# Attention on one core: the weighting and summing of three spans' exponentials moved from VectorE to TensorE and ScalarE

## The chip, the cores and the metric

The kernel runs on one core of a Trainium2 chip. The time is the device time of one execution in microseconds (us), from the first to the last instruction and what lies around them; the figure given for a kernel is the median of several runs.

## What is computed

The reference is a chain of six layers over eight images of 1024 tokens with 128 channels: a deformable convolution, a correlation layer that sorts each token's 1024 correlations, a windowed attention, a mixture of eight experts, a state space layer and a second mixture of experts. All is float32. The change is in the attention, which for each token looks at the last 4, 16 and 32 tokens:

```python
WINDOW_SIZES = (4, 16, 32)
q = hidden_states @ Wq + bq
contexts = []
for window in WINDOW_SIZES:
    patches = _gather_patches(hidden_states, window)
    keys = patches @ Wk + bk
    values = patches @ Wv + bv
    scores = jnp.einsum('bld,blwd->blw', q, keys) * scale
    attn = jax.nn.softmax(scores, axis=-1)
    contexts.append(jnp.einsum('blw,blwd->bld', attn, values))
merged = contexts[0]
for c in contexts[1:]:
    merged = merged + c
merged = merged / len(contexts)
return hidden_states + merged @ Wo + bo
```

## The kernel before

Tokens lie on the 128 partitions. An image is two halves of 512 tokens, four tiles of 128 each. Four chains of work run at the same time, each a Python generator per engine, and each engine runs its pieces strictly in the order in which they were written:

- F: the first layer of the next image (gathers by GpSimd, `diag` weights by ScalarE at L639, products by TensorE at L597), its normalization and the correlations of both halves (L623 to L630).
- S: the sort of one half (`dve_S`, L785 to L936). It is VectorE's alone. Its last instruction, L936, writes `tc`, the input of the attention of that half.
- C: attention, first expert layer and state space layer of one half, on TensorE, ScalarE and VectorE in turns. It runs under the sort of the next half. Its last instructions on VectorE are those of L1553, which write `tm`.
- M: the second expert layer of the two halves of the image before, one after the other (L1581 to L1713). VectorE multiplies there at L1713.

How the chains' pieces follow each other on an engine is a table of letters, `ORDER`, with a string for each engine and each kind of period: `fill`, `early`, `full`, `late` and `drain`. `weave` takes the next piece of the chain whose letter stands next. `full` is used for images 1 to 6 (images 2 to 6 are a loop on the chip). In such a period VectorE sorts the two halves of image i, the C chain does the second half of image i-1 and then the first half of image i, and the M chain does both halves of image i-1. In `drain` the sort is over, and the last half's C and M chains run out.

In the attention of a half, each tile's scores lie over 160 keys (32 past ones, `BACK`, and the tile's own 128). VectorE adds the three spans' bands and takes the minimum (L1126, L1128), in two parts p of two tiles each. ScalarE takes the exponentials into `sm` and their sums into `asum` (L1105). VectorE inverts the sums (L1133), multiplies the first span's exponentials by them (L1135) and adds the two others (L1140) into `prob`, whose first 96 columns ScalarE had set to zero (L1079). TensorE transposes `prob` in blocks of 128 x 128 (L1037), ScalarE copies the result to `prob_t` (L1111), and TensorE multiplies by the values `v_tok` of the tile and of the tile before (L1046, L1047). In the traces all of these tiles are `arena`, and PSUM tiles are `bank`.

## Time and profile before

| | |
|---|---|
| median of 3 runs | 4932.3 us (4931.25 to 4941.95) |
| profiled execution, its time | 4926.9 us |
| its span, first to last instruction | 4925.1 us |
| VectorE (DVE) busy | 4278.7 us, 87% of the span |
| TensorE (PE) busy | 3975.1 us, 81% |
| ScalarE (ACT) busy | 2954.3 us, 60% |
| GpSimd (POOL) busy | 894.7 us, 18% |
| mean granted TensorE clock | 0.893 |

Shares over the whole span mix the fill, the periods in which a sort runs, and the drain. The stretches are therefore to be read apart: the first sort starts at 249 us of the span and the last one ends at 4601 us.

### The profile page before, as it was taken

The page shows a single profiled execution, that of the slowest core. Times are in us where ns is not written, and L with a number is a line of the kernel's source. Part 1 is how long each engine was busy: PE and PEld are TensorE (multiplying, and loading weights), DVE is VectorE, ACT ScalarE, POOL GpSimd, SP SyncE. Part 2 cuts the span into 40 slices and gives each one's busy share as a digit, 9 for nine tenths or more (in the row PEclk, how much of TensorE's full clock was granted, in tenths as well). Part 3 has the DMA queues.
Part 4 walks back from the last instruction along what each step waited for, and adds up shares of the span by engine and source line. Part 5 has one row for each costly group of instructions (what it writes and reads, how often), then busy time and mean ns, then how long its engine had stood idle before and what let it go on. Part 6 is the DMA issues. An engine that isn't in the chain of part 4 may idle for free.

```text
span 4925.1 us, 59870 instructions
## 1 busy us (share of the span) xinstructions
PE 3975.1 (81%) x19410; PEld 2674.8 (54%) x19410; DVE 4278.7 (87%) x5380; ACT 2954.3 (60%) x7241; POOL 894.7 (18%) x580
## 2 busy tenths in 40 slices
PE   5747748989798988989798988989798987767587
PEld 3616424667456654567456654566456653545354
DVE  1098999999999999999999999999999999999521
ACT  4526526687467846687467846687467855555452
POOL 2317000242005300242005300242005210000000
PEclk8878869999899988999799988999799988978798
DMA  4314100232013210232013210232013210010001
GB/s 131 98 35 124 35 0 18 75 101 69 5 43 110 79 36 18 75 102 68 7 43 110 79 36 18 67 104 67 13 43 109 71 40 13 22 29 27 10 22 39
DMA packets 226079, 269.71 MB, mean 55 GB/s; under 512 B 26831, under 2 KB 188506, under 8 KB 225626
## 3 DMA queue, kind: packets, MB, share of 16 engines
q0 software_dynamic: 46080, 151.03, 10.6%
q1 hardware_dynamic: 179674, 114.65, 7.9%
q8 instruction: 167, 2.74, 0.2%
q14 instruction: 158, 1.29, 0.1%
HBM read 242.25 MB, written 23.34 MB: 54 GB/s over the span
## 4 chain that ended last, share of the span: by engine, by line
PE 38%; DVE 33%; issue 12%; ACT 9%; DMA 4%; POOL 3%; SPq 1%; DVEq 0%; another core or an unknown queue 0%; ACTq 0%; POOLq 0%
PE bank L597 6%; PE bank L1633 4%; PE bank L1628 4%; PE bank L1613 3%; PE bank L1298 3%; POOL gath L759 3%; DMA gath<-quads,idx 3%; DVE srt_b L873 2%; DVE srt_b L881 2%; DVE srt_a L796 2%; DVE srt_b L796 2%; PE bank L569 2%; PE bank L1225 2%; PE bank L1218 2%; DVE srt_a L893 2%
## 5 line engine op out<-in xcount | busy, mean ns | idle before, releaser
L759 POOL DMA_INDIRECT gath<-quads,idx x576 | 894.5, 1553 | 3083.4 <-DVE idx L722 2005.3
L597 PE MATMUL bank<-diag,gath 128*128 128x128 f32 x4608 | 612.4, 295 | 167.6 <-DMA gath<-quads,idx 166.8
L639 ACT ACTIVATE diag<-ident,w 128x128 f32<-128x128 f32 x2304 | 704.6, 393 | 20.3 <-DVE w L737 20.2
L597 PEld LDWEIGHTS bank<-diag,gath 128*128 128x128 f32 x4608 | 591.3, 210 | 203.1 <-DMA gath<-quads,idx 126.9
L1613 PEld LDWEIGHTS bank<-e2w,act 128*128 128x128 f32 (+1 forms) x3072 | 409.8, 198 | 161.7 <-issue 157.3
L1628 PE MATMUL bank<-mu_t,e2w 128*128 128x512 f32 (+1 forms) x768 | 424.0, 635 | 86.4 <-DMA e2w<-moe_w_t 39.9
L1633 PE MATMUL bank<-gated_u,e2w 128*128 128x512 f32 (+1 forms) x768 | 426.1, 638 | 34.2 <-DVE act L1713 31.9
L1713 DVE TENSOR_TENSOR act<-act,bank 128x512 f32<-128x512 f32 (+1 forms) x384 | 261.3, 680 | 180.0 <-PE bank L1633 159.5
L1613 PE MATMUL bank<-e2w,act 128*128 128x128 f32 (+1 forms) x3072 | 415.0, 282 | 1.6 <-DVE act L1713 1.6
L873 DVE TENSOR_TENSOR srt_b<-srt_a 128x1024 f32<-128x1024 f32 x192 | 351.3, 1830 | 1.2
L881 DVE TENSOR_TENSOR srt_b<-srt_a 128x1024 f32<-128x1024 f32 x192 | 351.0, 1828 | 0.0
L1681 ACT ACTIVATE act<-bank 128x512 f32<-128x512 f32 (+1 forms) x384 | 227.7, 593 | 201.5 <-PE bank L1628 198.8
L1681 ACT ACT_TABLE_LOAD x199 | 255.3, 1283 | 11.9 <-PE bank L1628 8.8
L672 ACT ACTIVATE cols<-bank 128x384 f32<-128x384 f32 x192 | 93.0, 484 | 245.1 <-PE bank L597 235.7
L1633 PEld LDWEIGHTS bank<-gated_u,e2w 128*128 128x128 f32 (+1 forms) x768 | 131.3, 188 | 186.7 <-issue 140.0
L794 DVE TENSOR_TENSOR srt_b<-srt_a 128x2048 f32<-128x2048 f32 x96 | 219.6, 2287 | 1.4
L794 DVE TENSOR_TENSOR srt_a<-srt_b 128x2048 f32<-128x2048 f32 x96 | 219.5, 2286 | 0.9
L796 DVE TENSOR_TENSOR srt_a<-srt_b 128x2048 f32<-128x2048 f32 x96 | 219.2, 2284 | 0.0
L796 DVE TENSOR_TENSOR srt_b<-srt_a 128x2048 f32<-128x2048 f32 x96 | 219.2, 2283 | 0.0
L901 DVE TENSOR_TENSOR srt_a<-srt_b 128x2016 f32<-128x2016 f32 (+1 forms) x96 | 211.8, 2206 | 0.9
L903 DVE TENSOR_TENSOR srt_a<-srt_b 128x2016 f32<-128x2016 f32 (+1 forms) x96 | 211.7, 2205 | 0.0
L1628 PEld LDWEIGHTS bank<-mu_t,e2w 128*128 128x128 f32 (+1 forms) x768 | 122.1, 188 | 148.3 <-issue 62.1
(348 smaller groups left out, 8161.5 us busy)
## 6 DMA issues: line engine op xcount, KB each, us to landing
e2w<-moe_w_t SPq DMA_DIRECT2D x256, 170.5 KB
quads<-xn_tok SPq DMA_DIRECT2D x256, 64.0 KB
e1w<-L_ffn_w SPq DMA_DIRECT2D x256, 64.0 KB, 1.9
e2w<-moe_w_t SPq DMA_DIRECT2D x256, 64.0 KB
gath<-quads,idx POOLq DMA_INDIRECT x576
e2w<-moe_w_t SPq DMA_DIRECT2D x128, 42.5 KB
x_tok<-x SPq DMA_DIRECT2D x8, 512.0 KB, 4.1
out<-tm SPq DMA_DIRECT2D x16, 256.0 KB, 2.3
```

What stands on the lines that cost most here:

```text
L597: ins = T.matmul(FB[q % 2][:, k * P:(k + 1) * P], gath[:, g % 2, k, s * C:(s + 1) * C], diag[:, g % 2, 4 * k + s], start=(s == 0), stop=(s ...
L639: ins = SC.activation(diag[:, g % 2, n], ident[:], ACT.Copy, scale=w[:, n:n + 1])
L759: pool.indirect_dma_start(gath[:, g % 2, k], None, quads, bass.IndirectOffsetOnAxis(idx[:, TG * g + k:TG * g + k + 1], 0)).then_inc(sem["g ...
L794: V.tensor_tensor(dst[:, :, 0:size // 2], lo, hi, ALU.max)
L796: return V.tensor_tensor(dst[:, :, size // 2:size], lo, hi, ALU.min)
L873: V.tensor_tensor(out_lo, lo, hi, ALU.max)
L881: link.put(V.tensor_tensor(out_hi, lo, hi, ALU.min))
L1613: ins = T.matmul(MB[2][:, t * P:(t + 1) * P], act2[0:m, n % ACT2_SLOTS, t * P:(t + 1) * P], e2w[0:m, e % 2, W2 + k * C:W2 + (k + 1) * C], ...
L1628: T.matmul(MB[r % 2][0:m, :], e2w[:, e % 2, k * P:k * P + m], mu_t[:], start=True, stop=True).then_inc(sem["m_ps"], 1)
L1633: T.matmul(MB[r % 2][0:m, :], e2w[:, e % 2, W3 + k * P:W3 + k * P + m], gated_u[:], start=True, stop=True).then_inc(sem["m_ps"], 1)
L1681: SC.activation(act2[0:m, n % ACT2_SLOTS], MB[r % 2][0:m, :], ACT.Silu).then_inc(sem["m_sb"], 1)
L1713: V.tensor_tensor(act2[0:m, n % ACT2_SLOTS], act2[0:m, n % ACT2_SLOTS], MB[r % 2][0:m, :], ALU.mult).then_inc(sem["hh"], 1)
```

## The change

VectorE keeps the reciprocals alone. ScalarE multiplies the identity by each tile's and span's reciprocals, which gives twelve diagonal matrices of 128 x 128 for a half (`pdiag`). TensorE multiplies the exponentials by these: with `sm` as the stationary operand and the diagonal as the moving one, the product is the weighted exponentials transposed, and three products added in PSUM are the sum over the spans. Since the past keys are now 32 rows, and no longer the last 32 of 128, the values of the tile before are needed at partitions 0 to 31. TensorE computes them a second time (`v_past`, four products with 32 columns of weights), and ScalarE copies them; the zeroing of `prob` falls away. The copy to `prob_t` becomes two copies for each part. Fourteen strings of the `ORDER` table, nearly all in which the C chain stands beside others, are new; the first line of one is shown.

```diff
     ACT_early=(
         "FFFFFFFFFFFFFFFFFFFFFFFFFFFFFFFFFFFFFFFFFFFFFFFFFFFFFFFFFFFFFFFFFFFFFFFFFFFFFFFFFFFFFFFFFFFFFFFF"
-        "FFFFFFFFFFFFFFCFFFFCCFFCFFCCCFFFFFCCFFFCCFCCFCCFFCCFFFFFFFFFFFFCCCCCCCCCCCCCCCCCCCCCCCCCCCCCCCCC"
+        "FFFFFFFFFFFFFFCFFFCFFCFFFCCCFFCFFCCCCFFCCFCCFCCFFCCFCFFFFFFFFFFCFCFCCCCCCCCCCCCCCCCCCCCCCCCCCCCCC"
...
-        v_halo = sb("v_halo", [P, C])
+        v_halo = sb("v_halo", [BACK, C])
...
-        prob = carve(UT * 2 * P, UT, 2 * P)
+        pdiag = carve(UT * NW * P, UT * NW, P)
+        v_past = carve(HALF, UT, C)
...
@@ pe_att
                 ins = T.matmul(CB[0][:, t * P:(t + 1) * P], utile(t), wqkvo[:, 2], start=True, stop=True)
             ins.then_inc(sem["qkv"], 1)
             yield
+            pe.wait_ge(sem["qkv_sb"], unit("qkv_sb", i, h, 3))
+            for t in range(UT):
+                ins = T.matmul(CB[0][0:BACK, t * P:(t + 1) * P], utile(t)[:, P - BACK:P], wqkvo[:, 2], start=True, stop=True)
+            ins.then_inc(sem["qkv"], 1)
+            yield
             pe.wait_ge(sem["qkv_sb"], unit("qkv_sb", i, h, 2))
...
                 pe.wait_ge(sem["probd"], unit("probd", i, h, p + 1))
                 if p == 0:
-                    pe.wait_ge(sem["prob_z"], unit("prob_z", i, h))
-                    pe.wait_ge(sem["qkv_sb"], unit("qkv_sb", i, h, 3))
-                for t in range(2):
-                    for s in range(2):
-                        ins = T.transpose(CB[p][:, (2 * t + s) * P:(2 * t + s + 1) * P], prob[:, 2 * p + t, s * P:(s + 1) * P], ident[:])
+                    pe.wait_ge(sem["qkv_sb"], unit("qkv_sb", i, h))
+                for t in range(2 * p, 2 * p + 2):
+                    for k, n, at in ((0, BACK, 0), (BACK, P, P)):
+                        for w in range(NW):
+                            ins = T.matmul(CB[p][0:n, t % 2 * 2 * P + at:t % 2 * 2 * P + at + P], sm[:, t, w, k:k + n],
+                                           pdiag[:, t * NW + w], start=(w == 0), stop=(w == NW - 1))
                 ins.then_inc(sem["prob_ps"], 1)
...
-                    past = v_tok[:, t - 1] if t else v_halo[:]
+                    past = v_past[0:BACK, t - 1] if t else v_halo[:]
                     if t or h:
-                        T.matmul(out, past, prob_t[:, t, 0:P], start=True, stop=False)
+                        T.matmul(out, past, prob_t[0:BACK, t, 0:P], start=True, stop=False)
@@ act_att
-            SC.activation(prob[:, :, 0:P - BACK], ident[:, 0:P - BACK].unsqueeze(1).to_broadcast([P, UT, P - BACK]), ACT.Identity,
-                          scale=0.0).then_inc(sem["prob_z"], 1)
-            yield
...
+            act.wait_ge(sem["qkv"], unit("qkv", i, h, 4))
             if h == 0:
-                SC.activation(v_halo[:], CB[0][:, HALF - P:HALF], ACT.Identity)
-            SC.activation(flat(v_tok), CB[0][:], ACT.Identity).then_inc(sem["qkv_sb"], 1)
+                SC.activation(v_halo[:], CB[0][0:BACK, HALF - P:HALF], ACT.Identity)
+            SC.activation(flat(v_past)[0:BACK], CB[0][0:BACK, :], ACT.Identity).then_inc(sem["qkv_sb"], 1)
             yield
...
             for p in range(2):
+                act.wait_ge(sem["arec"], unit("arec", i, h, p + 1))
+                for n in range(2 * NW * p, 2 * NW * (p + 1)):
+                    ins = SC.activation(pdiag[:, n], ident[:], ACT.Copy, scale=arec[:, n // NW, n % NW:n % NW + 1])
+                ins.then_inc(sem["probd"], 1)
+                yield
+            for p in range(2):
                 act.wait_ge(sem["prob_ps"], unit("prob_ps", i, h, p + 1))
-                SC.activation(flat(prob_t[:, 2 * p:2 * p + 2]), CB[p][:], ACT.Identity).then_inc(sem["prob_sb"], 1)
+                two = CB[p][:].rearrange("p (t s q) -> p t s q", t=2, s=2)
+                SC.activation(prob_t[0:BACK, 2 * p:2 * p + 2, 0:P], two[0:BACK, :, 0], ACT.Identity)
+                SC.activation(prob_t[:, 2 * p:2 * p + 2, P:2 * P], two[:, :, 1], ACT.Identity).then_inc(sem["prob_sb"], 1)
                 yield
@@ dve_att
                 dve.wait_ge(sem["expd"], unit("expd", i, h, p + 1))
-                two = range(2 * p, 2 * p + 2)
-                link(V.reciprocal(arec[:, 2 * p:2 * p + 2], asum[:, 2 * p:2 * p + 2]))
-                for t in two:
-                    ins = V.tensor_scalar(prob[:, t, P - BACK:2 * P], sm[:, t, 0], arec[:, t, 0:1], None, ALU.mult)
-                link(ins)
-                for w in (1, 2):
-                    for t in two:
-                        y = prob[:, t, P - BACK:2 * P]
-                        ins = V.scalar_tensor_tensor(y, sm[:, t, w], arec[:, t, w:w + 1], y, ALU.mult, ALU.add)
-                    if w == 1:
-                        link(ins)
-                ins.then_inc(sem["probd"], 1)
+                V.reciprocal(arec[:, 2 * p:2 * p + 2], asum[:, 2 * p:2 * p + 2]).then_inc(sem["arec"], 1)
                 yield
```

In the rows of the changed kernel below, line numbers are those of its own text. On VectorE, at the first attention of the loop's period (the second half of image i-1, under the sort of image i), the order before is this; L808 and L810 are pieces of the sort, L1126 and L1128 the bands and minima, L1133 to L1140 the weighting, and L1161 to L1163 the router of the M chain:

```order
L1126 TENSOR_TENSOR arena<-bank,band 128x960
...
L1128 TENSOR_REDUCE arena<-arena 128x6
...
L1161 SCALAR_TENSOR_TENSOR mgv<-moh,ml 128x32
...
L808 TENSOR_TENSOR corr<-srt_b 128x4x3x128
L810 TENSOR_TENSOR corr<-srt_b 128x4x3x128
L1133 RECIPROCAL arena<-arena 128x6
...
L1135 TENSOR_SCALAR arena<-arena 128x160 x2
...
L1140 SCALAR_TENSOR_TENSOR arena<-arena 128x160 x2
```

At the same place in the changed kernel (L809, L811, L795 and L797 are the sort, L1141 and L1143 the bands and minima, L1147 the reciprocals, L1156 and L1160 the router):

```order
L809 TENSOR_TENSOR corr<-srt_b 128x4x3x128
L811 TENSOR_TENSOR corr<-srt_b 128x4x3x128
...
L1141 TENSOR_TENSOR arena<-bank,band 128x960
...
L1143 TENSOR_REDUCE arena<-arena 128x6
L1156 TENSOR_REDUCE msm<-bank 128x4
...
L795 TENSOR_TENSOR srt_a<-corr 128x256x8
L797 TENSOR_TENSOR srt_a<-corr 128x256x8
L1147 RECIPROCAL arena<-arena 128x6
L1160 SCALAR_TENSOR_TENSOR mgv<-ml,rev 128x32
```

The multiplications are gone, the bands stand one pair of sort instructions later (L809 and L811), and the next pair (L795 and L797) stands ahead of the first reciprocal.

On TensorE, the same attention before, from the last projection (L1019) over the scores (L1026) and the transposes (L1037) to the first product with the values:

```order
L1019 MATMUL bank<-wqkvo,u_t 128x128 x4
L1022 ISA
L1026 MATMUL bank<-arena 128x160 x4
L1033 REGISTER_ALU
L1034 REGISTER_ALU
L1037 MATMUL bank<-ident,arena 128x128 x4
L1031 REGISTER_ALU
L1037 MATMUL bank<-ident,arena 128x128 x4
L1046 MATMUL bank<-arena,v_halo 128x128
```

And in the changed kernel (L1589 is the router product of the M chain, L1025 the past values, L1032 the scores, L1043 the products with the diagonals):

```order
L1020 MATMUL bank<-wqkvo,u_t 128x128 x4
L1589 MATMUL bank<-router,mu_t 128x8 x4
L1023 ISA
L1025 MATMUL bank<-wqkvo,u_t 32x128 x4
L1028 REGISTER_ALU
L1032 MATMUL bank<-arena 128x160 x4
L1039 REGISTER_ALU
L1043 MATMUL bank<-arena 32x128 x3
L1043 MATMUL bank<-arena 128x128 x3
```

The pair of L1043 rows comes four times in all. The past values stand ahead of the scores, and nothing of another chain stands between the scores and the products with the diagonals, as nothing stood ahead of the transposes.

On ScalarE, the same attention before, from the values (L1099) over the exponentials (L1105) to the copies of the transposed weights (L1111):

```order
L1099 ACTIVATE arena<-bank 128x512
L1105 ACTIVATE arena<-arena 128x160 x6
L1102 REGISTER_ALU
L1105 ACTIVATE arena<-arena 128x160 x6
L1111 ACTIVATE arena<-bank 128x512 x2
```

And in the changed kernel (L1106 copies the past values, L1119 makes the diagonals, L1658 is the M chain's exponential, L696 copies correlations of the F chain, L1125 and L1126 are the copies to `prob_t`):

```order
L1106 ACTIVATE arena<-bank 32x512
L1112 ACT_TABLE_LOAD
L1112 ACTIVATE arena<-arena 128x160 x6
L1109 REGISTER_ALU
L1112 ACTIVATE arena<-arena 128x160 x6
L1119 ACTIVATE arena<-ident,arena 128x128 x12
L1658 ACTIVATE mp<-ml 128x32
...
L696 ACTIVATE corr<-bank 128x4x128
...
L1125 ACTIVATE arena<-bank 32x2x128
L1126 ACTIVATE arena<-bank 128x2x128
```

The twelve diagonals stand between the exponentials and what ScalarE does next for the M and F chains. A table load stands at the exponentials. Over the whole loop body the number of table loads goes from 58 to 61, after the loop from 92 to 99, and ahead of it from 74 to 77.

## Rows read from the trace of the kernel before

**Rows 1.** The page, part 1: busy time, share of the span, instructions.

```profile
PE 3975.1 (81%) x19410; PEld 2674.8 (54%) x19410; DVE 4278.7 (87%) x5380; ACT 2954.3 (60%) x7241; POOL 894.7 (18%) x580
```

**Rows 2.** Windows from the first sort's start, then the drain; us, busy, TensorE's clock, DMA.

```profile
250.00:4600.00 4350.00, 3554.55 (x17412) 2385.07 (x17410) 4182.06 (x5120) 2671.99 (x6539) 826.30 (x504) 0.90 0.18 54
4600.00:4925.00 325.00, 262.08 (x1126) 167.21 (x1126) 78.82 (x216) 162.23 (x346) 0.00 (x0) 0.87 0.09 27
```

**Rows 3.** Windows, one period of the loop: PE, PEld, DVE, ACT, POOL busy.

```profile
2152.36:2708.80 556.44, 485.89 (x2427) 328.52 (x2426) 533.67 (x673) 370.64 (x909) 119.81 (x72) 0.92 0.21 59
```

**Rows 4.** Waits of DVE in that period: us in total, times, longest.

```profile
DVE act L1713 <- PE bank L1633: 5.3, 2, 5.1
DVE dtx L1476 <- ACT dtr L1404: 5.3, 2, 3.9
DVE mst L959 <- issue: 2.4, 1, 2.4
```

**Rows 5.** Timeline of DVE, ends of three sorts (L936) and of two C chains (L1553).

```profile
2372.28 0.86 DVE L1553 SCALAR_TENSOR_TENSOR tm<-bank,rms,td 128x128 f32<-128x128 f32 x3
...
2392.27 0.69 DVE L936 TENSOR_TENSOR tc<-x_tok,srt_a 128x512 f32<-128x512 f32 x1
...
2622.61 1.12 DVE L1553 SCALAR_TENSOR_TENSOR tm<-bank,rms,td 128x128 f32<-128x128 f32 x4
...
2682.61 0.69 DVE L936 TENSOR_TENSOR tc<-x_tok,srt_a 128x512 f32<-128x512 f32 x1
...
2948.85 0.69 DVE L936 TENSOR_TENSOR tc<-x_tok,srt_a 128x512 f32<-128x512 f32 x1
```

**Rows 6.** Groups by line, whole span: the weighting on DVE.

```profile
L1140 DVE SCALAR_TENSOR_TENSOR arena<-arena 128x160 f32<-128x160 f32 x128 | 43.5, 381 | 2.3
L1135 DVE TENSOR_SCALAR arena<-arena 128x160 f32<-128x160 f32 x64 | 16.5, 300 | 1.4
```

**Rows 7.** Timeline of DVE: both parts' reciprocals, and what follows.

```profile
2424.35 0.17 DVE L1133 RECIPROCAL arena<-arena 128x6 f32<-128x6 f32 x1
2424.57 0.51 DVE L1135 TENSOR_SCALAR arena<-arena 128x160 f32<-128x160 f32 x2
...
2426.43 0.18 DVE L1133 RECIPROCAL arena<-arena 128x6 f32<-128x6 f32 x1
...
2428.51 0.18 DVE L1166 TENSOR_TENSOR mgv<-mgv,rev 128x32 f32<-128x32 f32 x1
```

**Rows 8.** Timeline of PE at two attentions: transposes, products with values, output projection.

```profile
2426.75 1.11 PE L1037 MATMUL bank<-ident,arena 128*128 128x128 f32 x4 [13.66 <-DVE arena L1140]
...
2429.99 0.64 PE L1047 MATMUL bank<-arena 128*128 128x128 f32 x2
2430.41 0.63 PE L1046 MATMUL bank<-arena 128*128 128x128 f32 x2
...
2436.62 1.16 PE L1057 MATMUL bank<-wqkvo,arena 128*128 128x128 f32 x8
...
2721.52 0.39 PE L1047 MATMUL bank<-arena 128*128 128x128 f32 x2
2721.74 0.39 PE L1046 MATMUL bank<-arena 128*128 128x128 f32 x2
```

**Rows 9.** Windows around the first of these attentions, and behind it.

```profile
2400.00:2440.00 40.00, 23.10 (x83) 14.84 (x83) 39.29 (x64) 16.74 (x48) 0.00 (x0) 0.66 0.00 0
2440.00:2480.00 40.00, 39.00 (x154) 21.13 (x153) 39.21 (x58) 28.15 (x51) 0.00 (x0) 1.00 0.07 19
```

**Rows 10.** Timeline of ACT: twelve diagonals of the first layer, and a table load.

```profile
2689.57 1.28 ACT L1681 ACT_TABLE_LOAD   x1
...
2717.98 3.61 ACT L639 ACTIVATE diag<-ident,w 128x128 f32<-128x128 f32 x12
```

**Rows 11.** Groups by line, whole span: copies on ACT of the new shapes' kind.

```profile
L1403 ACT ACTIVATE arena<-bank 128x256 f32<-128x256 f32 x64 | 24.4, 382 | 2.1 <-PE bank L1300 1.6
L1409 ACT ACTIVATE arena<-bank 32x512 f32<-32x512 f32 x32 | 16.9, 574 | 2.5 <-PE bank L1306 2.5
```

83 lines of the change are left out of this document (43 added, 40 removed).

## The prediction

> **What bounds the kernel now.** The page's first part comes first: VectorE is busy for 87% of the span and TensorE for 81% [rows 1]. Two engines that close, averaged over stages with different limits, don't say which one decides, so the windows come next. From the first sort to the last VectorE is busy 4182 of 4350 us, 96%, and TensorE 3555, 82%; in the drain VectorE has 79 of 325 us and TensorE 262, 81% [rows 2]. In one period of the loop VectorE has 533.7 of 556.4 us, TensorE 485.9 (87%), ScalarE 370.6 (67%) [rows 3]. That leaves VectorE 22.7 us idle in a period. Its waits say what of: some 5 us in the expert product L1713 for TensorE, 5 us at the start of the state space layer for ScalarE, 2.4 us with no releaser shown [rows 4]; the rest is small. So the sort, with all that is threaded between its instructions, is the bound, and an instruction taken from VectorE there shortens the period, unless a wait fills the place.
>
> The second question is how much room the other chains have. A half's C chain starts at L936 and ends at L1553. One ends at about 2373.1 where the next starts at 2392.3, the next at 2623.7 where the following starts at 2682.6 [rows 5]. So C is ahead of the sort by 19 us in one half and by 59 in the other.
>
> **What VectorE loses.** The groups give 43.5 + 16.5 = 60.0 us for 16 attentions, 3.75 us each [rows 6]. The timeline checks that with the gaps in it: from one reciprocal to the next 2.08 us, of which the reciprocal itself, start to next start, is 0.22, so 1.86 for a part and 3.7 for a half; the second part, 2426.43 to 2428.51, gives the same [rows 7]. Fifteen of the sixteen attentions lie under a sort: 15 x 3.7 = 56 us. The sixteenth lies in the drain, where VectorE is not the bound. For a period it is 7.4 us, 1.3% of 556.4.
>
> **What TensorE gains.** A float32 product of 128 columns is two records in the trace, a transpose one: L1057 stands four times in the order and eight times in the timeline, L1037 four and four [rows 8]. A half's eight transposes become 24 products with diagonals, and four products for the past values come: 48 + 8 - 8 = 48 records more. The trace has no 32-column weights of this kind; I take them at the price of 128, because the moving side, 128 columns, is the same. Bounds from the same rows: two records from 2721.52 to 2721.74, so 0.11 us each, and from 2429.99 to 2430.41, so 0.21 each [rows 8]. That is 5.3 to 10.1 us for a half, 10.6 to 20.2 in a period. I take 13: the granted clock was 0.92 over a period, but 0.66 around the attention at 2400 to 2440 [rows 3, 9], which is a stretch in which most of it ran at 1.2 GHz after a wait of 13.7 us for the weighting [rows 8]. TensorE then has about 499 us in a period of about 550, 91% instead of 87%. The waiting place itself takes part of that in: nothing else stood between scores and transposes before, and nothing does now. But just behind it, from 2440, TensorE has 39.0 of 40 us [rows 9]; whatever runs beyond the wait is late there, and with it L1713 on VectorE with the sort queued behind it.
>
> **What ScalarE gains.** Twelve diagonals take 3.6 us (L639, same shape, scale from a column [rows 10]). The copy of the past values is 0.57 [rows 11]; two smaller copies, by the 0.38 of a 256-column copy [rows 11], take the place of one in each part, about 0.3 more for a half. The zeroing that falls away is left out of the sum. Table loads go from 456 to 481 executed (77 + 5 x 61 + 99 against 74 + 5 x 58 + 92), each 1.28 us [rows 10]: 3.8 us in a period. All in all about 2 x 4.5 + 3.8 = 13 us in a period, 384 of 550 us, 70%. No bound, but a lateness: behind the diagonals stand the copies of the F chain's correlations.
>
> Taken together the three engines have more to do than before: VectorE's 3.7 us for a half become 3.6 on ScalarE and 5 or more on TensorE. If the sum were what counts, with all of the 13 us of TensorE on the path and 7.4 gone, the period would grow by 5.6 us and the time by 7.5 x 5.6 + 6 = 48, to about 4980. The windows speak against it, since the three are busy at the same time and only one is full [rows 2, 3].
>
> The Trainium skill, "ScalarE: Activation LUTs" (section Rules for kernel authors), says to put a multiplication on VectorE and not on ScalarE; by that rule the change goes the wrong way, to the slower time just worked out. The rows agree that ScalarE is no faster at it here, but the rule looks at one instruction, not at which queue is full.
>
> **The attention's own latency.** After the last exponential there were two weightings of 2.1 us and transposes; now come 1.8 us of diagonals for each part and 24 records of products for each part, 2.7 to 5.1 us. And the scores wait for the copy of the values and the past values' eight records, 0.6 + 0.9 us or more. About 6 us more in all where nothing covers it. Under a sort it is covered: the order has moved the bands and the reciprocals behind one more pair of sort instructions each, and C has 19 and 59 us of lead [rows 5]. Without that cover each half would be later by those 6 us, 12 in a period. In the drain nothing covers it: the last half's C chain, and M behind it, are the end. There I take +6 us, between 0 (M work of the other half fills TensorE) and 12 (lower clock, and some of the added table loads).
>
> **The sum.** The profiled execution took 4926.9 us for a span of 4925.1. Saved -56; drain +6; and growth of VectorE's waits on TensorE and ScalarE in the 15 half periods, unknown. Its lower bound is nothing (the wait at the transposes takes all of the added work), its upper bound all of the 13 us of a period, which is 98 over seven and a half periods. The nearest row is VectorE's own wait on TensorE, 5.3 us in a period at 87% [rows 4]; with TensorE's idle time down from 70 to about 50 us I let it grow by some 1.5 us, together 11. That gives 4926.9 - 56 + 6 + 11 = 4888. The profiled run lies 5.4 us below the median of 4932.3, inside the scatter of the runs; half of that is added: **4890 us**, 0.9% faster.
>
> **The rivals.**
> - *All of it comes through.* VectorE's waits stay as they are, since the new order was laid for the new costs. For it: the lead of C, and that the waits in a period are few and short. Against: TensorE's share. 4932.3 - 56 + 6 = 4882, or down to 4870 if the drain costs nothing and a wait or two falls away too. This lies so near my forecast that I count them together: 0.72.
> - *TensorE takes it back.* Of the 13 us added in a period some 7 reach VectorE as waits at L1713 and at the C chain's products; the time stays within 10 us of 4932. For it: 39.0 of 40 us busy right behind the attention [rows 9]. Against: 70 us of idle time in a period. 0.14.
> - *Slower: the products with diagonals run at the lower clock behind a longer wait.* Place: the first attention of each period, where the diagonals come later than the weighting did and TensorE has nothing else in between. Price: 10.1 us there and about 8 in the other half, 18 in a period; if two thirds pass on, 12 - 7.4 = 4.6 a period, 7.5 x 4.6 + 6 = +40, 4972; with all of TensorE's 13 us passed on, the 4980 worked out above. It decides from 7.4 us passed on, 41% of the 18. For it the clock of 0.66 [rows 9]; against it that the 13.7 us of waiting were there already and cost VectorE nothing. 0.10.
> - *The order does something else.* With fourteen strings new, another wait (the correlations, the gathers) may move by more than the change itself, either way. 0.04.
>
> **The numbers.** What a measurement of this kernel can tell from no change is about 0.2%, 10 us. Forecast and first rival reach from 4866 to 4920; the range goes on into the second, to 4936, and leaves out the third and the best tail. Faster 0.78 (the first case, a part of the second and the last), same 0.10, slower 0.12.
>
> **What would show it.** Right: a loop period of about 550 us between ends of sorts (L936's counterpart); VectorE's weighting gone with a reciprocal of 0.2 us left, and its busy time lower by some 60 us; 48 more PE records for each half; the added work behind the scores without new waits at the bands or the sort's L809. Wrong: waits of VectorE on TensorE at the expert product of more than 12 us in a period, a sort that waits for its correlations, or a period of 556 or more with VectorE's share down to 94%. A drain of more than 337 us would show the latency mis-sized.

## The result and the profile after

The changed kernel takes **4976.8 us**, the median of 4 runs (4973.57 to 4982.57), against 4931.8 (4931.01 to 4941.95) for the kernel before beside it: a ratio of 1.0094, interval 1.0079 to 1.011. It is 0.9% slower. The forecast was 0.9% faster, 4890 us, with a range up to 4936: sign and range were both wrong.

The page of the changed kernel, part 1, and the first line of part 4 (the chain that ended last, shares by engine); the second fence is that line in the page of before:

```profile
PE 4064.4 (82%) x20178; PEld 2741.7 (55%) x20178; DVE 4226.5 (85%) x5188; ACT 3043.2 (61%) x7490; POOL 944.7 (19%) x580
...
PE 46%; DVE 28%; issue 10%; ACT 8%; DMA 4%; POOL 2%; SPq 1%; DVEq 0%; ACTq 0%; POOLq 0%
```

```profile
PE 38%; DVE 33%; issue 12%; ACT 9%; DMA 4%; POOL 3%; SPq 1%; DVEq 0%; another core or an unknown queue 0%; ACTq 0%; POOLq 0%
```

VectorE's busy time fell by 52 us against [rows 1], TensorE's rose by 89, ScalarE's by 89. The span grew from 4925.1 to 4971.7. The chain has moved: TensorE's share of it went from 38 to 46%, VectorE's from 33 to 28%. That line of the page of before was there to be read before the forecast. It covers the whole span, with the fill and the drain, in which VectorE has little to do. Summed over the stretch with sorts alone, the chain of before has VectorE at 36% and TensorE at 35%; over four periods in the middle it has TensorE at 46% and VectorE at 21%, though VectorE is the fuller of the two there. What such a share is worth the experiments show.

Windows of the changed kernel, the counterparts of [rows 2, 9] and of one loop period [rows 3]: us, busy of PE, PEld, DVE, ACT, POOL (instructions), TensorE's granted clock, DMA share and GB/s:

```profile
249.00:4642.00 4393.00, 3639.10 (x18132) 2449.61 (x18130) 4134.42 (x4942) 2757.22 (x6774) 876.31 (x504) 0.90 0.18 53
4642.00:4967.00 325.00, 266.66 (x1165) 168.96 (x1166) 74.46 (x202) 165.52 (x359) 0.00 (x0) 0.89 0.09 26
...
2147.92:2708.04 560.12, 491.98 (x2524) 333.37 (x2524) 526.91 (x648) 380.38 (x938) 126.95 (x72) 0.94 0.20 59
2420.00:2460.00 40.00, 19.73 (x86) 12.46 (x86) 39.29 (x63) 20.51 (x61) 0.00 (x0) 0.79 0.01 2
2460.00:2500.00 40.00, 39.72 (x160) 22.37 (x160) 37.55 (x61) 25.28 (x48) 0.00 (x0) 1.00 0.00 0
```

The stretch from the first sort to the last grew from about 4351 to 4393 us while VectorE's busy time in it fell from 4182 to 4134: its idle time there went from 168 to 259 us. The loss is therefore in the sorted part. The drain, last sort end to end of span, is 324.1 us before and 329.6 after. Over the four periods in the middle (ends of sorts 6 to 14) the trace of before gives a mean of 557.1 us a period with VectorE idle for 23.7, the trace after 562.3 with 35.4. So VectorE gave up 6.4 us of work in a period and took on 11.6 of waiting. The 47 us by which the spans differ lie so: 18 ahead of the end of the sixth sort (1836.7 us before, 1854.4 after), 21 in the four middle periods, 2 in the last two sorts, 5.5 in the drain.

What it waits for, over the whole span, after and then before (us in total, times, longest):

```profile
DVE act L1717 <- PE bank L1637: 153.9, 59, 14.1
DVE act L1717 <- ACT act L1685: 67.5, 19, 7.6
...
DVE lnst L960 <- ACT tbu L1132: 32.8, 11, 14.2
DVE lnsd L1080 <- ACT lnsd L1070: 27.1, 8, 21.4
```

```profile
DVE act L1713 <- PE bank L1633: 159.5, 49, 15.9
DVE act L1713 <- ACT act L1681: 17.0, 18, 2.8
DVE lnsd L1073 <- ACT lnsd L1063: 14.7, 2, 13.2
...
DVE lnst L959 <- ACT tbu L1117: 9.6, 1, 9.6
```

(L1717, L1637, L1685, L960, L1132, L1080 after are L1713, L1633, L1681, L959, L1117, L1073 before.) Two waits carry most of the growth over the span. The expert product waits for ScalarE's activation, 17.0 to 67.5 us; and the normalization behind the attention waits for the attention's output (L1132), 9.6 to 32.8. The second is the attention's own lateness, arriving at VectorE.

At the first attention of the loop's period, on VectorE (L1141 and L1143 bands and minima, L1147 reciprocals, L937 end of a sort, L1557 end of a C chain; compare [rows 5, 7]):

```profile
2401.25 1.12 DVE L1557 SCALAR_TENSOR_TENSOR tm<-bank,rms,td 128x128 f32<-128x128 f32 x4
...
2416.73 0.69 DVE L937 TENSOR_TENSOR tc<-x_tok,srt_a 128x512 f32<-128x512 f32 x1
...
2446.61 1.15 DVE L1143 TENSOR_REDUCE arena<-arena 128x6 f32<-128x960 f32 x1
...
2452.40 0.18 DVE L1147 RECIPROCAL arena<-arena 128x6 f32<-128x6 f32 x1
...
2453.01 0.18 DVE L1147 RECIPROCAL arena<-arena 128x6 f32<-128x6 f32 x1
```

On ScalarE, and then on TensorE, at that place (compare [rows 8]):

```profile
2452.62 3.61 ACT L1119 ACTIVATE arena<-ident,arena 128x128 f32<-128x128 f32 x12 [2.03 <-DVE arena L1147]
...
2469.82 0.60 ACT L1132 ACTIVATE tbu<-bank 128x512 f32<-128x512 f32 x1 [2.10 <-PE bank L1064]
```

```profile
2436.86 1.06 PE L1025 MATMUL bank<-wqkvo,u_t 128*32 128x128 f32 x8
2437.85 1.35 PE L1032 MATMUL bank<-arena 128*128 128x160 f32 x8
2454.61 7.99 PE L1043 MATMUL bank<-arena 128*32 128x128 f32 x48 [15.40 <-ACT arena L1119]
2462.52 0.48 PE L1053 MATMUL bank<-arena,v_halo 32*128 32x128 f32 x2
```

The last exponential ends at 2450.6, ScalarE waits 2 us for the reciprocal, makes twelve diagonals in 3.61 us as forecast, and TensorE, after 15.4 us of waiting, needs 8.0 us for the 48 records of products. From the first reciprocal to the attention's output it is 18.0 us; before, 14.1 (2424.35 to 2438.4). From the end of the sort (2417.4) to that output it is 53.0 us, and 45.5 before.

This is the quickest of the four first attentions in the middle periods. Over the four, the products take 8.0 to 9.5 us, 9.0 in the mean, and 7.5 at the second attentions. From the first reciprocal to the output the means are 19.9 us at the first attention and 18.7 at the second, before 14.0 and 18.1.

### The profile page after: what moved, and what is told of

Its sections match the earlier page's. It is cut to its first block, busy times and chain, and to the rows that moved or that the text cites. A ratio compares the mean times of both kernels' runs of the same rounds, so it can differ in the third digit from the quotient of the medians.

```text
span 4971.7 us, 61384 instructions
## 1 busy us (share of the span) xinstructions
PE 4064.4 (82%) x20178; PEld 2741.7 (55%) x20178; DVE 4226.5 (85%) x5188; ACT 3043.2 (61%) x7490; POOL 944.7 (19%) x580
## 3 DMA queue, kind: packets, MB, share of 16 engines
q0 software_dynamic: 46080, 151.03, 10.7%
## 4 chain that ended last, share of the span: by engine, by line
PE 46%; DVE 28%; issue 10%; ACT 8%; DMA 4%; POOL 2%; SPq 1%; DVEq 0%; ACTq 0%; POOLq 0%
PE bank L598 7%; PE bank L1617 4%; PE bank L1632 4%; PE bank L1637 4%; PE bank L1302 3%; DMA gath<-quads,idx 3%; PE bank L1043 2%; PE bank L608 2%; PE bank L1344 2%; DVE srt_a L797 2%; PE bank L570 2%; DVE srt_a L894 2%; POOL gath L760 2%; DVE srt_a L795 2%; DVE srt_b L797 2%
## 5 line engine op out<-in xcount | busy, mean ns | idle before, releaser
L760 POOL DMA_INDIRECT gath<-quads,idx x576 | 944.5, 1640 | 3073.6 <-DVE idx L723 2043.4
L1637 PE MATMUL bank<-gated_u,e2w 128*128 128x512 f32 (+1 forms) x768 | 425.9, 638 | 73.1 <-DVE act L1717 72.1
L1717 DVE TENSOR_TENSOR act<-act,bank 128x512 f32<-128x512 f32 (+1 forms) x384 | 261.3, 680 | 223.5 <-PE bank L1637 153.9
L1685 ACT ACTIVATE act<-bank 128x512 f32<-128x512 f32 (+1 forms) x384 | 228.4, 595 | 198.9 <-PE bank L1632 195.2
L1637 PEld LDWEIGHTS bank<-gated_u,e2w 128*128 128x128 f32 (+1 forms) x768 | 129.9, 188 | 241.1 <-issue 150.4
L1043 PE MATMUL bank<-arena 128*32 128x128 f32 (+1 forms) x768 | 131.1, 327 | 124.6 <-ACT arena L1119 124.6
L795 DVE TENSOR_TENSOR srt_b<-srt_a 128x2048 f32<-128x2048 f32 x96 | 219.6, 2288 | 1.3
L795 DVE TENSOR_TENSOR srt_a<-srt_b 128x2048 f32<-128x2048 f32 x96 | 219.4, 2286 | 0.8
L797 DVE TENSOR_TENSOR srt_b<-srt_a 128x2048 f32<-128x2048 f32 x96 | 219.4, 2285 | 0.0
L797 DVE TENSOR_TENSOR srt_a<-srt_b 128x2048 f32<-128x2048 f32 x96 | 219.3, 2284 | 0.0
```

Source lines behind the costliest of these rows:

```text
L760: pool.indirect_dma_start(gath[:, g % 2, k], None, quads, bass.IndirectOffsetOnAxis(idx[:, TG * g + k:TG * g + k + 1], 0)).then_inc(sem["g ...
L795: V.tensor_tensor(dst[:, :, 0:size // 2], lo, hi, ALU.max)
L797: return V.tensor_tensor(dst[:, :, size // 2:size], lo, hi, ALU.min)
L1637: T.matmul(MB[r % 2][0:m, :], e2w[:, e % 2, W3 + k * P:W3 + k * P + m], gated_u[:], start=True, stop=True).then_inc(sem["m_ps"], 1)
L1685: SC.activation(act2[0:m, n % ACT2_SLOTS], MB[r % 2][0:m, :], ACT.Silu).then_inc(sem["m_sb"], 1)
L1717: V.tensor_tensor(act2[0:m, n % ACT2_SLOTS], act2[0:m, n % ACT2_SLOTS], MB[r % 2][0:m, :], ALU.mult).then_inc(sem["hh"], 1)
```

## The experiments

Unless said otherwise an edit is against the kernel before. "Period", "idle" and "drain" are worked out from each trace as above, over the same four periods. Ratios are to the kernel before, run beside each; its medians there were 4928.1 us (7 runs; beside work and order, VectorE alone, and the 48 records behind the wait), 4924.8 (14 runs; beside the 48 at the attention's end, ScalarE alone, scores first, and half the products) and 4931.4 (25 runs; beside the other three). Differences in us are taken from these. The periods and waits of a kernel come from its one traced execution. It lies within 6 us of the median of its runs, except for old work in the new order (16 us above) and scores first (13 above). Theory A of the expectations is that the order table alone is at fault; theory B is that the added work is, in any order.

### Work and order taken apart

New work in the old order: the changed kernel with the strings of before, in which each new piece stands right behind the piece it follows. As an example, ScalarE's string of the loop:

```diff
-        "CMFFCMCMCCCCCCCCMFFCCCMCFMMCFFCMMCFMFCFM...
+        "FFMCMMCMCCCCCCCCCCCCFFCMFMMCFFMMCMFCCMMF...
```

> The changed attention with the order table of the kernel before; the new pieces are threaded in right behind the piece they follow (the past values behind the values, the diagonals behind the exponentials). Theory A (the new order table lost the time, the work itself is a gain): 4875 to 4900 us, a loop period near 550. Theory B (the added work of TensorE and ScalarE costs VectorE more waiting than it saves, under any order): 4955 or more, period 561 or more.

Measured: 5053.2 us, 1.0244 (1.0218 to 1.0269), on the side of theory B. Period 569.8, VectorE idle 43.5 in it. Its waits on VectorE over the whole span:

```profile
DVE act L1717 <- PE bank L1637: 223.4, 65, 15.9
...
DVE lnst L960 <- ACT tbu L1132: 76.3, 16, 12.2
```

Old work in the new order: the attention of before with the strings of the changed kernel, less the pieces that it doesn't have.

```diff
-        "FFMCMMCCMCCCCCCCCCFFCMFMMCFFMMCMFCCMMFFM...
+        "CMFFCCMCMCCCCCMFFCCCMCFMMCFFCMMCFMFCFMFF...
```

> The attention of the kernel before with the changed kernel's order table, the letters of the pieces that don't exist left out. Theory A: at least 4975 us, since VectorE has the 56 us of weighting back on top of a bad order (up to 5030). Theory B: near 4932, since the added work is gone.

Measured: 4959.4 us, 1.0061 (1.0043 to 1.0079), between the two theories, which had 4975 or more and about 4932. Period 564.3, VectorE idle 30.6; the attention's output comes 51 to 54 us behind the sort's end though the work is the old. In one period on VectorE:

```profile
DVE act L1713 <- ACT act L1681: 7.2, 1, 7.2
DVE arena L1539 <- PE bank L1361: 5.9, 4, 3.5
```

What follows: the order alone costs 31 us (21 to 39 by its interval), the work in the old order 125, both together 45. (In the first of these kernels the diagonals stand directly behind the exponentials on ScalarE, ahead of what the old order had there; a part of its loss may be that.) So the table is not the culprit by itself: in it the work still costs 17 us more (4959.4 to 4976.8, with intervals that just touch). It makes room for the new work, as the wait for L1132 goes from 76 to 33 us. But it pays for that by laying the attention later, and most of the 45 us is there with the old work already.

The loop shows the same. The expert product's wait for ScalarE's activation is 8.1 us a period in the changed kernel, 7.3 with the old work in the new order (6.6 to 7.9 in each of the four), and 1.1 in the kernel before. VectorE is idle for 35.4, 30.6 and 23.7 us. Of the 11.6 us of growth about 7 thus come with the order, somewhat less if that trace is slower than its kernel usually is, and about 5 with the work. TensorE's wait at the first attention's transposes is longer in this table with the old work too: 14.9 to 17.9 us in the four periods, against 13.7 to 13.8 in the kernel before. Whether another table could avoid both costs is not shown.

### VectorE's share alone

The second and third span are neither weighted nor added.

```diff
                     ins = V.tensor_scalar(prob[:, t, P - BACK:2 * P], sm[:, t, 0], arec[:, t, 0:1], None, ALU.mult)
-                link(ins)
-                for w in (1, 2):
-                    for t in two:
-                        y = prob[:, t, P - BACK:2 * P]
-                        ins = V.scalar_tensor_tensor(y, sm[:, t, w], arec[:, t, w:w + 1], y, ALU.mult, ALU.add)
...
                 ins.then_inc(sem["probd"], 1)
```

> The kernel before with the second and third span not weighted and not added (that part of the computation is left out): VectorE loses 2.7 us for a half and nothing is added elsewhere. If VectorE is the bound as I read it: 15 x 2.7 = 41 us less, 4888 to 4896. If VectorE's waits take it back under an unchanged order: above 4915.

Measured: 4892.0 us, 0.9931 (0.9915 to 0.9948), as expected of VectorE as the bound. Period 551.5, VectorE idle 23.5 in it, as before. 41 us forecast, 36 got, by the medians. The reading that what is taken from VectorE in the sorted part comes off the time is right. It is the rest of the change that took the gain.

### TensorE's work, at three places

The same 48 records of 128 columns a half, added to the kernel before, at three places. First behind the wait for the weighting, ahead of the transposes of each part:

```diff
+                for n in range(12):
+                    T.matmul(CB[p][:, n % 4 * P:(n % 4 + 1) * P], sm[:, 2 * p + n % 2, n % 3, BACK:BACK + P], ident[:], start=True, stop=True)
                 for t in range(2):
                     for s in range(2):
```

> The kernel before with 24 products (48 records) more ahead of each half's transposes, whose results are overwritten: the added TensorE work alone, VectorE unchanged. Theory A: it is taken in by the wait at the transposes and by idle time, 4932 to 4955 us. Theory B: most of 13 us in a period reaches VectorE, 5000 us or more.

Measured: 4983.4 us, 1.012 (1.0101 to 1.0139), between the theories (up to 4955, and 5000 or more); period 562.3, VectorE idle 28.6.

Second, behind the last product of the attention, where nothing in the attention waits for them:

```diff
             ins.then_inc(sem["att_out"], 1)
+            for n in range(24):
+                T.matmul(CB[1][:, n % 4 * P:(n % 4 + 1) * P], wqkvo[:, n % 3], ident[:], start=True, stop=True)
             yield
```

> The kernel before with the same number of extra records (24 products, 48 records a half), but behind the attention's last product instead of ahead of its transposes, so that the attention itself isn't later. Theory C (what costs is that the attention's result comes later on TensorE, into a VectorE order that has placed the next step just in time): 4930 to 4950 us. Theory D (TensorE's own time costs, wherever it stands, since all chains pass through its queue): about as much as ahead of the transposes, 4970 to 4990.

Measured: 4987.7 us, 1.0128 (1.0107 to 1.015), theory D's range; period 564.0, VectorE idle 30.3.

Third, between the scores and the wait for the weighting:

```diff
+            pe.wait_ge(sem["qkv_sb"], unit("qkv_sb", i, h, 3))
+            for n in range(24):
+                T.matmul(CB[0][:, n % 4 * P:(n % 4 + 1) * P], wqkvo[:, n % 3], ident[:], start=True, stop=True)
             for p in range(2):
                 pe.wait_ge(sem["probd"], unit("probd", i, h, p + 1))
...
-                    pe.wait_ge(sem["qkv_sb"], unit("qkv_sb", i, h, 3))
```

> The kernel before with the same 48 records a half more, now between the scores and the wait for the weighting, where TensorE is idle for 13.7 us at the first attention of a period and 1.6 at the second. Behind that wait (e3) they cost 55 us, at the attention's end (f1) 63. Theory E (TensorE's own time is the period's length but for some 70 us of idle time that lies where its queue has nothing it may do; only work placed inside such a wait is free): the first attention's share vanishes, 4940 to 4965. Theory F (any record more costs its time, wherever it stands): 4978 to 4992.

Measured: 4942.5 us (10 runs, 4932.85 to 4951.12), 1.0025 (1.0014 to 1.0035), in theory E's range and far from theory F's; period 555.3, VectorE idle 22.0, the drain 332.0.

TensorE at the same attention in these three, in the order told. The first, with the products (L1036) and transposes (L1039):

```profile
2463.75 4.42 PE L1036 MATMUL bank<-ident,arena 128*128 128x128 f32 x24 [12.89 <-DVE arena L1142]
2468.01 0.60 PE L1039 MATMUL bank<-ident,arena 128*128 128x128 f32 x4
2468.45 2.84 PE L1036 MATMUL bank<-ident,arena 128*128 128x128 f32 x24
```

The second, with the transposes (L1037) and, behind the output projection, the products (L1060):

```profile
2451.77 1.11 PE L1037 MATMUL bank<-ident,arena 128*128 128x128 f32 x4 [13.49 <-DVE arena L1142]
...
2461.43 5.52 PE L1060 MATMUL bank<-ident,wqkvo 128*128 128x128 f32 x48
```

The third, with the products (L1032) ahead of the wait:

```profile
2426.55 5.52 PE L1032 MATMUL bank<-ident,wqkvo 128*128 128x128 f32 x48
2440.47 1.11 PE L1039 MATMUL bank<-ident,arena 128*128 128x128 f32 x4 [8.39 <-DVE arena L1142]
```

Only in the third does the wait shrink, from 13.66 [rows 8] to 8.39 us, by 5.3 for 5.5 us of products. Over the middle periods TensorE's waits at the transposes of both halves go from 16.8 to 8.9 us a period, and its idle time from 72.0 to 64.6. There the waiting place takes the work in, and the loop pays nothing. The 11 us that this version costs lie elsewhere: the sixth sort ends 14 us later, and the drain is 8 longer. In the first the wait is still 12.9 and everything behind it is later by what was added. The second shows that it isn't the attention's own latency alone: its attention is as quick as before (table below), and still 63 us are lost, 3.9 for each of 16 halves out of 5.5 of work. What is left to be hit there is what follows on TensorE in its fixed order, the products of the other chains. It also shows that a lower clock is not needed for the loss: these 48 records ran at 0.115 us each, the quicker of the two prices [rows 8].

None of the three costs all that was added. At 0.115 us a record the 48 are 88 us over sixteen halves; 55, 63 and 11 came through. And TensorE's busy time grew less than the records took in all three: by 6.3, 6.6 and 5.7 us a period, for 14.5, 11.0 and 11.0 us of records. The granted clock moved with it. It was at the lower of its two levels for 87 us of a period in the kernel before, and for 78, 78 and 70 in these, and the other products ran faster.

### ScalarE's work alone

Twelve diagonals a half that nobody reads, behind the exponentials, in the kernel before.

```diff
+        pdiag = carve(UT * NW * P, UT * NW, P)
...
                 ins.then_inc(sem["expd"], 1)
+                if p:
+                    for n in range(UT * NW):
+                        SC.activation(pdiag[:, n], ident[:], ACT.Copy, scale=bqk[:, 0:1])
                 yield
```

> The kernel before with twelve diagonals a half on ScalarE behind the second part's exponentials, unused: ScalarE's added work alone, where the change has it. At the first attention of a period ScalarE waited 6.7 us there for the transposes, at the second it had M's work next. Theory C: up to 3.6 us later at each second attention, 4940 to 4960. Theory D: it costs next to nothing, since ScalarE is at 67%: 4928 to 4938.

Measured: 4947.4 us, 1.0047 (1.0031 to 1.0063), +23: theory C's range, but not its place. The middle periods are no longer than before (556.2, idle 22.7). The sixth sort ends 11.7 us later, and the drain is 6 us longer. ScalarE's diagonals, when nothing waits for them, are hidden in the loop and cost in the first periods and at the end.

### Taking parts out of the changed kernel

Scores ahead of the past values, so that the bands on VectorE can come earlier (the edit swaps the two blocks in `pe_att`, against the changed kernel):

```diff
-            pe.wait_ge(sem["qkv_sb"], unit("qkv_sb", i, h, 3))
-            for t in range(UT):
-                ins = T.matmul(CB[0][0:BACK, t * P:(t + 1) * P], utile(t)[:, P - BACK:P], wqkvo[:, 2], start=True, stop=True)
-            ins.then_inc(sem["qkv"], 1)
-            yield
             pe.wait_ge(sem["qkv_sb"], unit("qkv_sb", i, h, 2))
```

> The changed kernel with the scores ahead of the past values on TensorE, so that bands, exponentials and diagonals can start some 1.6 us earlier. The work is the same. Theory C: 10 to 20 us less than the changed kernel's 4977. Theory D: 4972 to 4980, no difference.

Measured: 4968.4 us, 1.0081 (1.0059 to 1.0102). 8 us less than the changed kernel by the medians, with intervals that overlap and just short of both expected ranges: inconclusive, and small in any case.

Half of the products with diagonals (those for the 32 past keys) left out, against the changed kernel:

```diff
-                    for k, n, at in ((0, BACK, 0), (BACK, P, P)):
+                    for k, n, at in ((BACK, P, P),):
```

> The changed kernel without the products for the 32 past keys (that part of the weights is left out, what lies in PSUM is copied): 24 records a half less on TensorE. If TensorE's time passes on as it did in the kernel before with 48 records more (+55 us): 25 us less, 4945 to 4958. If the new order had made room for it: 4970 or more.

Measured: 4930.1 us (10 runs, 4917.22 to 4943.73), 1.0005 (0.999 to 1.002); period 558.2, VectorE idle 31.5. 24 records a half fewer give back 47 us, where 25 were expected. That is 3 for each half, for 4.0 us of work at the 0.166 us of a record in the changed kernel's row (7.99 us for 48). In the new order too, TensorE's added work is not covered.

Four diagonals a half in place of twelve, against the changed kernel:

```diff
-                                           pdiag[:, t * NW + w], start=(w == 0), stop=(w == NW - 1))
+                                           pdiag[:, t * NW], start=(w == 0), stop=(w == NW - 1))
...
-                for n in range(2 * NW * p, 2 * NW * (p + 1)):
+                for n in range(2 * NW * p, 2 * NW * (p + 1), NW):
```

> The changed kernel with four diagonals a half instead of twelve, each used for all three spans (two of three weightings are left out of the computation): ScalarE loses 2.5 us a half, 39 over all, and the products may start earlier; TensorE's work and the order as in the changed kernel. At the 40% that ScalarE's work alone cost in the kernel before: 16 us less, 4955 to 4965. If ScalarE's time stands wholly in the chain: 4938. If not at all: 4973 or more.

Measured: 4945.8 us (10 runs, 4928.46 to 4959.63), 1.0027 (1.0012 to 1.0042); period 560.3. 31 us less than the changed kernel for 39 us of ScalarE's work: more than the 16 expected, less than all. 14 of it lie ahead of the end of the sixth sort, and a middle period is 2 us shorter. Diagonals that the products wait for cost in the loop; the same diagonals beside the path were hidden there.

### TensorE's work taken out of the kernel before

The three products of 512 columns that add residual and bias to the attention's output left out, 41 us of TensorE in all, against the kernel before.

```diff
-            T.matmul(CB[0][:], ident[:], flat(tc[:]), start=True, stop=False)
-            T.matmul(CB[0][:], ident[:], flat(u), start=False, stop=False)
-            T.matmul(CB[0][:], ones[0:1, :], row4(bo_row[:]), start=False, stop=False)
             yield
             pe.wait_ge(sem["ctx_sb"], unit("ctx_sb", i, h))
...
```

> The kernel before without the two residual products and the bias product of the attention's output (that part of the computation is left out): 6 records of 512 columns a half less on TensorE, 2.6 us, 41 us over sixteen; VectorE and ScalarE as before. Theory E: TensorE's time is in the bound, so the time falls by 30 to 45 us, 4883 to 4898, though VectorE is at 96%. If VectorE were the bound, as I had it: 4920 to 4930, no gain but in the drain.

Measured: 4930.7 us (10 runs), 1.0005 (0.999 to 1.002); period 558.1. TensorE's busy time falls from 485.1 to 479.1 us a period, its idle time rises from 72.0 to 79.0, and the time stays. That refutes Theory E in its full form, by which the period was TensorE's busy time and a fixed 70 us of waiting; its other half, that work inside a wait is free, stands by the run before. The place matters here too. The products that were left out stand ahead of the wait for ScalarE's copy of the context. Nothing waited there before, and now TensorE does:

```profile
2441.27 1.16 PE L1054 MATMUL bank<-wqkvo,arena 128*128 128x128 f32 x8 [0.69 <-ACT arena L1111]
```

That is 1.4 us in a period, of the 5.1 taken out by the estimate above; the rest went into other waits. So work that was added behind a wait passed on, and this work, taken out ahead of one, did not. Taking work out behind the wait of the kernel before was not tried.

The middle periods of all kernels, means over four periods in us (att: from a sort's end to the attention's output, at the first and second attention of a period; sort 6: when the sixth sort ends):

| | time | sort 6 | period | PE busy | DVE busy | DVE idle | att | drain |
|---|---|---|---|---|---|---|---|---|
| before | 4931.8 | 1836.7 | 557.1 | 485.1 | 533.4 | 23.7 | 45.4, 48.0 | 324.1 |
| after | 4976.8 | 1854.4 | 562.3 | 494.4 | 527.0 | 35.4 | 54.9, 52.3 | 329.6 |
| new work, old order | 5053.2 | 1886.9 | 569.8 | 498.8 | 526.3 | 43.5 | 51.4, 58.0 | 333.6 |
| old work, new order | 4959.4 | 1855.6 | 564.3 | 483.2 | 533.7 | 30.6 | 54.2, 51.5 | 320.1 |
| less on VectorE only | 4892.0 | 1825.5 | 551.5 | 482.5 | 527.9 | 23.5 | 42.3, 48.4 | 323.2 |
| 48 records behind the wait | 4983.4 | 1867.0 | 562.3 | 491.4 | 533.8 | 28.6 | 48.4, 53.8 | 320.7 |
| 48 at the attention's end | 4987.7 | 1857.1 | 564.0 | 491.7 | 533.7 | 30.3 | 44.7, 48.2 | 331.0 |
| 48 ahead of the wait | 4942.5 | 1850.7 | 555.3 | 490.8 | 533.3 | 22.0 | 45.0, 48.5 | 332.0 |
| diagonals, unused | 4947.4 | 1848.4 | 556.2 | 482.8 | 533.5 | 22.7 | 44.9, 50.8 | 330.3 |
| residual products out | 4930.7 | 1842.7 | 558.1 | 479.1 | 533.6 | 24.5 | 42.4, 49.0 | 319.3 |
| after, scores first | 4968.4 | 1858.9 | 563.1 | 494.0 | 527.0 | 36.1 | 54.4, 51.7 | 329.8 |
| after, half the products | 4930.1 | 1844.8 | 558.2 | 487.4 | 526.7 | 31.5 | 51.4, 50.9 | 326.6 |
| after, 4 diagonals | 4945.8 | 1840.2 | 560.3 | 492.5 | 526.7 | 33.6 | 52.3, 51.0 | 326.1 |

## Why the prediction was wrong

**What bounds the kernel: right as far as it went.** VectorE leads in the kernel before; 36 of 41 us taken from it came off the time, and 41 us taken from TensorE brought nothing. What was missing is that the lead is thin. The chain of the page, which the prediction did not use, had TensorE at 38% and VectorE at 33% over the whole span.

**What VectorE loses: right.** 7.4 us forecast in a period; its busy time is 6.4 lower.

**What TensorE gains: the size a little low, the placing was a failure.** 48 records a half more came (20178 - 19410 = 768 = 16 x 48). In a middle period the new records take 18.5 us and the transposes took 3.6: 15 us more, against 13 forecast and inside the bounds of 10.6 to 20.2. Busy time grew by only 9.3, since the rest of TensorE's work ran faster, at a mean granted clock of 0.93 against 0.92. But the sentence "The waiting place itself takes part of that in" failed. The wait at L1043 is a wait for the diagonals, and the products need the diagonals: they stand behind it and can't fill it. It did not shrink but grew, 13.66 to 15.40 us at the first attention; the growth itself is the order's, as the old work in the new order waits 14.9 to 17.9 us there. The same records cost 11 us ahead of the wait, 55 behind it and 63 at the attention's end. The forecast had added the work of one side of a wait to the room on the other.

**What ScalarE gains: the size near, "No bound, but a lateness" half right.** Busy time grew by 10.7 us in a period against 13. Alone it costs 23 us, outside the middle periods; in the changed kernel two thirds of the diagonals are worth 31 us, where TensorE waits for them.

**The attention's own latency: right in size, wrong in "Under a sort it is covered".** From reciprocal to output it grew by 5.9 us at the first attention and 0.6 at the second, and from sort end to output by 9.5 and 4.3, of which the order alone brings 8.8 and 3.5 (table). The cover was read from C's lead at its end, 19 and 59 us [rows 5]. In the changed kernel that lead is still 15 and 58 (2402.4 to 2417.4, and 2650.0 to 2708.0). A lead at the end of a chain is no slack of its parts. Each part is waited for on the other engines by pieces in a fixed order, here by the normalization L960 and by the expert product L1717. When those are late the sort behind them is late too, so that the lead stays.

**The sum: the failed step.** Its term for the growth of VectorE's waits was 1.5 us a period, 11 in all, taken from a row of 5.3 us [rows 4] and TensorE's 70 idle us. Measured, VectorE's idle time grew by 11.6 a period, near the upper bound of 13 that the prediction gave beside it. About 7 of these come with the new order table, whose cost the sum had nowhere, and about 5 with the work in it. With the measured terms the sum comes out, which is bookkeeping and no proof: (11.6 - 6.4) x 7.5 = 39, and 5.5 for the drain, 45 against the 47 by which the spans differ.

From the experiments the parts are: +31 for the order (old work in it), and +17 for the work in that order. In it, half of the products are worth 47 us and two thirds of the diagonals 31. In the old order they are -36 for VectorE's second and third span, and up to 15 more for the first, which that run kept (16.5 us [rows 6], 15 of 16 under a sort), if it passes on as well; +55 to +63 for TensorE; +23 for ScalarE. That is +27 to +50. It must not be held against the measured 45, which contains another order; its counterpart is the +125 of the new work in the old order. So the parts do not add up there, and where the other 75 us or more come from is open. What the parts do show is their sign: TensorE's added work alone, 55 to 63 us, costs more than VectorE's saved work brings, 36 to 51. (The lower end of the stated range, 4866, has no working; the case that it belongs to went down to 4870.)

**The drain: agrees.** +6 forecast, +5.5 measured, by one trace of each kernel; with the old attention in the new order it was 4 shorter than before.

**The rivals.** "All of it comes through" is refuted. "TensorE takes it back" named the right place and too small a part. "Slower" came out in time, 4972 or, with all of TensorE's work passed on, 4980; measured 4976.8. Its place was right in part (a longer wait, then all of the products), its reason only in part: the products took 9.0 us there in the mean, between the 5.3 and the 10.1 of its two prices, and the products at the attention's end lost as much with every record at the quick price. That its number was met owes something to luck, as it had no term for the order. "The order does something else", with a chance of 0.04, describes the other part: the order alone costs 31 of the 45 us, and the wait that grew most in the loop hangs on a gather, as shown below. Of the signs of being wrong, one came: a period of 562 us with VectorE's share at 94%. The wait at the expert product came to 10.2 us in a period, under the 12 named, and only 2.1 of it were on TensorE, the rest on ScalarE. The Trainium skill, "ScalarE: Activation LUTs" (section Rules for kernel authors), whose rule puts a multiplication on VectorE, gave the slower time of 4980 in the prediction; this case's measurement agrees with that side, though what it shows as the larger part of the added work's cost is TensorE's products, of which the rule says nothing.

One wait shows how the engines hold each other up. Late in the second sort of the period in the changed kernel, on TensorE, ScalarE and VectorE in turn:

```profile
2668.41 4.95 PE L598 MATMUL bank<-diag,gath 128*128 128x128 f32 x24 [5.79 <-DMA gath<-quads,idx]
...
2673.40 0.49 ACT L673 ACTIVATE cols<-bank 128x384 f32<-128x384 f32 x1 [10.39 <-PE bank L598]
...
2676.82 0.69 DVE L1717 TENSOR_TENSOR act<-act,bank 128x512 f32<-128x512 f32 x1 [7.28 <-ACT act L1685]
```

TensorE waits for a gather of the next image. ScalarE waits for TensorE to copy the columns, and the activation of the expert layer stands behind that copy. VectorE waits for the activation with the sort behind it. None of the three belongs to the attention. In the kernel before the gather is 2.9 us late at this place, and VectorE waits there for TensorE's product, 5.1 us [rows 4]. With the old work in the new order the same wait is there in full, on TensorE and on VectorE:

```profile
2673.32 4.88 PE L597 MATMUL bank<-diag,gath 128*128 128x128 f32 x24 [5.56 <-DMA gath<-quads,idx]
...
2681.66 0.69 DVE L1713 TENSOR_TENSOR act<-act,bank 128x512 f32<-128x512 f32 x1 [7.17 <-ACT act L1681]
```

So this wait is the order's and not the new work's.

What stays open: through which chain the 63 us of the products at the attention's end reach VectorE (the gathers, the expert layer and the state space layer are all behind them on TensorE), why the parts do not add up in the old order, and how much of the new order's 31 us could be had back by another table for the same work. No version tried beat the kernel before and computed the whole attention.

## What to carry to other kernels

Room in front of a wait is only room for work that does not need what is waited for. Before adding work to an engine that has idle time, ask on which side of its waits the work must stand. Behind them, with the queues in fixed order and the leading engine at 96%, some two thirds of it came through here although TensorE was idle for 13% of the period; ahead of them, an eighth. Test a new order with the old work in it before charging a loss to the work: here it was 31 of 45 us. And read the chain of the page besides the busy shares, as a warning and not as a price. It ran over a second engine for as long as over the fullest, and added work on that engine cost. But over the middle periods it had TensorE at 46% and VectorE at 21%, and still it was VectorE's time that came off in full (5.6 us a period for 5.4 taken out) and TensorE's that did not.

## What the runs showed of the hardware that was not expected

The 32-column weights of the past values cost what weights of 128 columns do, 1.06 us for eight records against 1.05 for the values' eight. Loading them took less, 0.110 against 0.192 us in the median of the weight loads of those two lines (L1025, L1020), but the products' pace did not show it. The products of a half took 0.166 us a record behind the wait of 15.4 us, between the two levels, with a granted clock of 0.79 from 2420 to 2460 and 1.00 from 2460 to 2500; with 48 records in front of the wait in the kernel before, the transposes behind the wait of 8.39 us still ran at the lower clock (1.11 us for four), so that a wait filled with 5.5 us of products did not keep the clock up. More work on TensorE did raise its clock elsewhere. In the changed kernel the new records took 18.5 us of a middle period, the transposes in the kernel before 3.6, and yet TensorE's busy time grew by 9.3 only: everything else on it took 5.6 us less, with the lower level granted for 74 us of a period in place of 87. 41 us taken from TensorE bought nothing, and 88 us added behind a wait or at the attention's end cost 55 to 63.
